# Landmark phase as a three-stage pipeline over images with 32-row score tiles

## What is computed

```
x = x + lstm(group_norm(x))
t = tokens(x)
a = layer_norm(t);  xn = layer_norm(a) * gamma + beta
q, k, v = split(xn @ w_qkv)
q_l, k_l = means of q and k over 64 segments of 64 tokens
out = softmax(q k_l') @ pinv(softmax(q_l k_l')) @ (softmax(q_l k') @ v)
out = (out + depthwise_conv(v)) @ w_out + b_out
t = t + a + out
t = t + ffn_recurrence(layer_norm(t))
```

## Time and profile before

| | us |
|---|---|
| median of three runs | 7382.85 (7371.74 to 7390.95) |
| the profiled execution's own time | 7392.79 |
| its span | 7391.1 |
| landmark phase, 1612 to 3246 us of the span | 1634 |
| pinv phase, to 3628 us | 382 |
| output phase, to 5060 us | 1432 |
| recurrence, to the end | 2331 |

### The profile page before, as it was taken

The page is one execution under the profiler, slowest core; times in us unless marked ns, Lnnn a source line. Parts: engine busy times, 40 slices in busy tenths (PEclk is TensorE's granted clock), DMA queues, the critical chain, the costliest instruction groups (busy, mean ns, idle before and its releaser), DMA issues. The chain is left out here.

```text
span 7391.1 us, 234424 instructions
## 1 busy us (share of the span) xinstructions
PE 6762.3 (91%) x93297; PEld 3741.3 (51%) x93297; DVE 3505.2 (47%) x9371; ACT 3435.6 (46%) x9744; POOL 1775.4 (24%) x1718
## 2 busy tenths in 40 slices
PE   4599999978888898889899999997999999999999
PEld 3499888973333343459544444443333333333333
DVE  7677777767667777734266666662000000000000
ACT  4465555655555555524355555553333333333333
POOL 1000000015666766630044444441000000000000
PEclk6799999988999999989899999998999999999999
DMA  6521111233444433310144444442111111111111
GB/s 273 231 95 68 69 69 46 93 108 123 138 138 138 138 128 119 98 51 0 54 154 151 153 152 147 152 138 62 42 52 52 41 54 41 52 41 52 45 50 41
DMA packets 749351, 711.30 MB, mean 96 GB/s; under 512 B 61168, under 2 KB 655088, under 8 KB 741104
## 3 DMA queue, kind: packets, MB, share of 16 engines
q1 hardware_dynamic: 733872, 594.91, 25.7%
q0 software_dynamic: 14400, 101.45, 3.4%
HBM read 388.50 MB, written 305.80 MB: 94 GB/s over the span
## 5 line engine op out<-in xcount | busy, mean ns | idle before, releaser
L2060 PE MATMUL f_junk<-f_idle 128*32 128x384 bf16 x24736 | 1565.1, 323 | 1.5 <-issue 1.3
L2103 ACT ACTIVATE f_y<-f_acc 128x16 f32<-128x16 f32 x4096 | 753.7, 184 | 1555.6 <-PE f_acc L2071 1555.5
L2071 PEld LDWEIGHTS f_acc<-f_y,f_vT 128*32 128x32 f32 x32768 | 649.2, 108 | 1415.0 <-ACT f_y L2103 1403.2
L2071 PE MATMUL f_acc<-f_y,f_vT 128*32 128x16 f32 x32768 | 1049.6, 193 | 60.7 <-issue 12.2
L2018 DVE TENSOR_TENSOR f_sum<-f_turned,f_t 128x512 f32<-128x512 f32 x128 | 88.6, 692 | 1769.0 <-PE f_turned L2053 1768.9
L695 POOL TENSOR_TENSOR a_acc<-a_acc,a_p 128x512 f32<-128x512 f32 x480 | 617.5, 1287 | 350.2 <-ACT a_p L898 345.4
L898 ACT ACTIVATE a_p<-a_s 128x512 f32<-128x512 f32 x512 | 300.5, 590 | 638.8 <-PE a_s L826 596.0
L825 PE MATMUL a_s<-a_ws,a_xnT 128*128 128x512 f32 x1024 | 568.8, 638 | 22.3 <-issue 19.8
L1789 DVE TENSOR_REDUCE o_m<-o_bank_l 128x8 f32<-128x512 f32 x512 | 326.1, 679 | 413.7 <-PE o_bank_l L1591 413.5
L2060 PEld LDWEIGHTS f_junk<-f_idle 128*32 128x32 bf16 x24736 | 446.4, 96 | 3.6 <-issue 3.6
L999 DVE TENSOR_REDUCE a_m3p<-a_l 128x1 f32<-128x512 f32 x512 | 319.1, 684 | 143.7 <-PE a_l L766 141.8
(11 more groups left out here) (251 smaller groups left out, 13385.4 us busy)
## 6 DMA issues: line engine op xcount, KB each, us to landing
a_hid<-hidden SPq DMA_DIRECT2D x16, 4127.5 KB, 13.4
hidden<-l_h POOLq DMA_DIRECT2D x48, 1040.0 KB, 6.3
skew<-gn_skew POOLq DMA_DIRECT2D x8, 6144.0 KB, 23.8
l_x<-skew SPq DMA_DIRECT2D x48, 1024.0 KB, 5.2
gn_x<-in_x SPq DMA_DIRECT2D x16, 2048.0 KB, 12.3
a_xin<-in_x SPq DMA_DIRECT2D x128, 256.0 KB, 6.7
base<-a_t SPq DMA_DIRECT2D x16, 2048.0 KB, 8.8
xnt<-a_xnT SPq DMA_DIRECT2D x16, 2048.0 KB, 14.0
```

The lines of the kernel that those rows point to most:

```text
L2060: nc.tensor.matmul(junk[rows, :], idle[:, 0:QUAD], idle[:, :], start=True, stop=True)
L2071: mm = nc.tensor.matmul(acc[k % 2][rows, t, :], vT[:, rows], before, start=False, stop=True, skip_group_check=True)
L2103: nc.scalar.activation(y[q][:, u, :], acc[u // RC % 2][:, u % RC, :], ACT.Sigmoid).then_inc(s_y, 1)
```

## The change

`landmark_phase` is rewritten. Time is cut into `B + 2` = 18 periods of eight slots, and three images are in work at once. In period `p`, slot `c`, group `c` of image `p` is added and normalised (its transposes, keys and values are one slot later), the landmarks and the rounded maxima belong to image `p-1`, and the scores, exponentials and weighing to image `p-2`.

- Keys are now formed (`keys`, one 512-column float32 product per group) and kept as `kT`. A score is a product over the 32 channels of two heads: four tiles of 32 rows, one for each pair of heads, each into its own bank. A group takes 4 bf16 products for the shift and 16 float32 products of 128 columns. The product `w_k @ qbd` and the four-row shift are gone.
- The values are stored 17 wide per head with a one in the last place, so that a row of the weighing is the softmax's sum. POOL's adding into `acc` is gone. The weighing has 8 products of 64 columns per tile (before: 4 of 128).
- The norm is made by POOL alone (five operations, two of 512 elements), which also keeps `gain` and `loss` for each tile. DVE's L936, L937, L946, L951, L952 and ACT's L876 and POOL's L682 are gone; `tokens` (the unscaled `t`) goes to memory in place of `base`. POOL also rounds the keys; ACT's L870 is gone.
- The two transposes share one bank `turn` (before: two), keys and values share `proj`, and the rounded products and all small landmark products share one bank `L` (before: two banks and `misc`).
- Transfers are cut into groups of 512 tokens and eight pieces of the hidden rows, each issued in its slot by SP.
- In `output_phase`, the add of `base` (one 128x512 operation) becomes four operations of 128 columns with `gain`, a wait, and four with `loss` and `b_out`. The convolution reads its values 17 apart.

The core of the diff follows (marks of removed lines are left out for `landmark_phase`, whose old text stands above).

```diff
+        LAST = {1: 0, 2: 6, 3: 12, 4: 18, 5: 23, 6: 28, 7: 32}
+        ROUNDED = {1: range(0, 3), 2: range(3, 4), 3: range(4, 5), 4: range(5, 7), 5: range(7, 8)}
...
+        def before(p, c):
+            return (p, c - 1) if c else (p - 1, NG - 1)
...
+            def slot(p, c, q):
+                more = valid(p + 1)
+                if valid(p):
+                    if c in (1, 3, 5) and more:
+                        load_hidden(p + 1, c // 2)
+                    if c == NG - 1 and more:
+                        for piece in range(3, 8):
+                            load_hidden(p + 1, piece)
+                    if c + 3 < NG:
+                        load_x(p, c + 3)
+                    elif more:
+                        load_x(p + 1, c + 3 - NG)
+                i, d = before(p, c)
+                if valid(i):
+                    store_normed(i, d)
+                if valid(p):
+                    store_tokens(p, c)
+                if valid(i):
+                    store_values(i, d, q if c else 1 - q)
...
+            def norm(i, c):
+                n = nth(i, c) - 1
+                mean = mv[c % 2][:, :, 0]
+                var = mv[c % 2][:, :, 1].unsqueeze(1).broadcast_to([P, 2, GT])
+                wait(pool, "bn", n + 1)
+                pool.tensor_tensor(vare[:, :, :], var, coef[:, :, :], ALU.mult).then_inc(s["pow"], 1)
+                pool.wait_ge(s["pow"], 6 * n + 1)
+                pool.tensor_tensor(vare[:, :, :], vare[:, :, :], plus[:, :, :], ALU.add).then_inc(s["pow"], 1)
+                wait(pool, "xt", n)
+                pool.tensor_tensor(xn[:, :, :], t[c % 2][:, :, :], mv[c % 2][:, :, 0:1].broadcast_to([P, GT, C]), ALU.subtract
+                                   ).then_inc(s["pow"], 1)
+                pool.wait_ge(s["pow"], 6 * n + 3)
+                pool.tensor_tensor(r[:, :, :], vare[:, :, :], half[:, :, :], ALU.pow).then_inc(s["pow"], 1)
+                pool.wait_ge(s["pow"], 6 * n + 4)
+                pool.tensor_tensor(xn[:, :, :], xn[:, :, :], r[:, 1, :].unsqueeze(2).broadcast_to([P, GT, C]), ALU.mult
+                                   ).then_inc(s["xn"], 1)
+                tiles = slice(GT * c, GT * c + GT)
+                pool.tensor_tensor(R.gain[:, bass.ds(i, 1), tiles], r[:, 0:1, :], one[:, :].unsqueeze(2).broadcast_to([P, 1, GT]),
+                                   ALU.add).then_inc(s["pow"], 1)
+                pool.tensor_tensor(R.loss[:, bass.ds(i, 1), tiles], r[:, 0:1, :], mean.unsqueeze(1), ALU.mult
+                                   ).then_inc(s["pow"], 1)
+            def round_keys(i, j, q):
+                wait(pool, "kc", nth(i, j))
+                wait(pool, "lp", NL * i + PAIRS_H * (j - 2) if j >= 3 else NL * i)
+                pool.tensor_tensor(k_lp[j % 3][:, :], kT[q][:, 512 * j:512 * j + 512], one[:, :].broadcast_to([C, 512]), ALU.mult
+                                   ).then_inc(s["rk"], 1)
+            def slot(p, c, q):
+                if valid(p):
+                    norm(p, c)
+                if valid(p - 1):
+                    for j in ROUNDED.get(c, ()):
+                        round_keys(p - 1, j, 1 - q)
+            each_period(pool, slot)
...
+            def turn_hidden(i, c):
+                wait(pe, "hc", nth(i, c))
+                if isinstance(i, int) and nth(i, c) == 2:
+                    wait(pe, "add", 1)
+                wait(pe, "xnT", nth(i, c) - 2)
                 for k in range(GT):
+                    mt = nc.tensor.transpose(turn[:, k, :], hrow[c % 2][:, P * k:P * k + P], R.ident[:, :])
+                mt.then_inc(s["ht"], 1)
+            def turn_normed(i, c):
+                wait(pe, "xn", nth(i, c))
+                wait(pe, "add", min(nth(i, c) + 1, NG * B) if isinstance(i, int) else nth(i, c) + 1)
                 for k in range(GT):
...
+            def keys(i, c):
+                wait(pe, "xnT", nth(i, c))
+                wait(pe, "valc", nth(i, c) - 1)
+                nc.tensor.matmul(proj[:, :], w[:, C:2 * C], xnT[c % 4][:, :], start=True, stop=True).then_inc(s["km"], 1)
+            def values(i, c):
+                wait(pe, "kc", nth(i, c))
+                for k in range(GT):
+                    mt = nc.tensor.matmul(proj[:, P * k:P * k + P], xnT[c % 4][:, P * k:P * k + P], w[:, 2 * C:3 * C],
+                                          start=True, stop=True)
+                mt.then_inc(s["vm"], 1)
...
+            def rounded_scores(i, j):
+                if j % PAIRS_H == 0:
+                    wait(pe, "rk", NG * i + j // PAIRS_H + 1)
                 if j == 0:
...
+            def turn_maxima(i):
+                wait(pe, "set", SET * i + 11)
+                nc.tensor.transpose(L[:, 0:P], m3[:, :], R.ident[:, :]).then_inc(s["lm"], 1)
+            def scores(i, c, q):
+                wait(pe, "exp", PAIRS_H * (nth(i, c) - 1))
+                if c == 0:
+                    wait(pe, "set", SET * (i + 1))
+                for g in range(PAIRS_H):
+                    rows = slice(QUAD * g, QUAD * g + QUAD)
+                    nc.tensor.matmul(S[g][:, :], sel[rows, :], m3row[q][rows, :].unsqueeze(1).broadcast_to([QUAD, GT, P]),
+                                     start=True, stop=False)
                 for k in range(GT):
+                    at = 512 * c + P * k
+                    for g in range(PAIRS_H):
+                        rows = slice(QUAD * g, QUAD * g + QUAD)
+                        ms = nc.tensor.matmul(S[g][:, P * k:P * k + P], kT[q][rows, at:at + P], qbd[q][rows, P * g:P * g + P],
+                                              start=False, stop=k == GT - 1)
+                ms.then_inc(s["s"], 1)
+            def weigh(i, c, q):
+                wait(pe, "exp", PAIRS_H * nth(i, c))
+                if c == 0:
+                    wait(pe, "ctx", CTX * (i - 1) + 1)
+                for k in range(GT):
+                    for h in range(2):
+                        for g in range(PAIRS_H):
+                            at = VROW * (GT * c + k) + (DH + 1) * (2 * g + h)
+                            mw = nc.tensor.matmul(pv[QUAD * g:QUAD * g + QUAD, LM * h:LM * h + LM], v[q][:, at:at + QUAD],
+                                                  p3[c % 2][g][:, P * k + LM * h:P * k + LM * h + LM],
+                                                  start=c == 0 and k == 0 and h == 0, stop=c == NG - 1 and k == GT - 1,
+                                                  skip_group_check=True)
+                mw.then_inc(s["pvd"], 1)
+            def context(i):
+                wait(pe, "ctx", CTX * i + 1)
+                nc.tensor.transpose(L[:, 0:P], pvs[:, :], R.ident[:, :]).then_inc(s["turnc"], 1)
+            def slot(p, c, q):
+                i, d = before(p, c)
+                due = list(range(LAST.get(c - 1, 0), LAST.get(c, 0))) if valid(p - 1) else []
+                def rounded():
+                    if due:
+                        rounded_scores(p - 1, due.pop(0))
+                if valid(p - 2):
+                    scores(p - 2, c, q)
+                if c == 1 and valid(p - 1):
+                    landmarks(p - 1)
+                rounded()
+                if valid(p):
+                    turn_hidden(p, c)
+                rounded()
+                j, e = before(p - 2, c)
+                if valid(j):
+                    weigh(j, e, q if c else 1 - q)
+                rounded()
+                if valid(i):
+                    turn_normed(i, d)
+                rounded()
+                if c == 0 and valid(p - 3):
+                    context(p - 3)
+                if valid(i):
+                    keys(i, d)
+                rounded()
+                if valid(i):
+                    values(i, d)
+                rounded()
+                if c == 1 and valid(p - 1):
+                    landmark_scores(p - 1, 1 - q)
+                if c == NG - 1 and valid(p - 1):
+                    turn_maxima(p - 1)
...
+            def copy_normed(i, c):
+                wait(act, "xt", nth(i, c))
+                stored(act, s_stx, nth(i, c) - 4)
+                wait(act, "xm", nth(i, c) - 4)
+                wait(act, "vm", nth(i, c) - 4)
+                nc.scalar.activation(xnT[c % 4][:, :], turn[:, :, :].rearrange("c k t -> c (k t)"), ACT.Identity,
+                                     bias=bet[:, 0:1], scale=gam[:, 0:1]).then_inc(s["xnT"], 1)
+            def copy_keys(i, c, q):
+                wait(act, "km", nth(i, c))
+                wait(act, "s", nth(i - 2, c))
+                wait(act, "rk", nth(i - 2, c))
+                nc.scalar.activation(kT[q][:, 512 * c:512 * c + 512], proj[:, :], ACT.Identity).then_inc(s["kc"], 1)
+            def copy_values(i, c, q):
+                wait(act, "vm", nth(i, c))
+                wait(act, "pvd", nth(i - 2, c))
+                stored(act, s_stv, nth(i - 2, c))
+                nc.scalar.activation(v[q][:, GT * VROW * c:GT * VROW * (c + 1)].rearrange("p (a d) -> p a d", d=DH + 1)[:, :, 0:DH],
```

(81 more changed lines are left out.)

665 lines of the change are left out of this document (221 added, 444 removed).

## The result

The changed kernel takes 7435.53 us, median of four runs (7419.61 to 7437.80), against 7381.83 (7371.74 to 7390.95, four runs) for the kernel before: a ratio of 1.0068 [1.0049, 1.0088]. It is 0.7% slower, where 7223 us was predicted. The profiled execution took 7435.45 us, its span 7433.7.

What follows compares the result with a forecast made beforehand. PE was taken to bound the landmark phase, a chain over all engines the output phase's slots. From 7392.8 us, -314 (landmark) and +154 (output) gave 7233 profiled, 7223 as median; range 7010 to 7370 us.

Steps and rivals of the forecast that it cites:

- landmark phase: Landmark phase: all periods with opening and closing sum to 1320 us against 1634 before, 314 less.
- two blocks, delay only: Output phase: two blocks for the add make `z` later, slots 11.6 us instead of 10.41, +154 us over 127 slots.
- the forecast 75%: Sign in the landmark phase: PE's busy share near 75%.
- the opening and the closing: Ends of the landmark phase: opening 13 us, period 16 52, period 17 and tail 38; good to some 20 us together.
- the sum that gave 78: Landmark image: 73.8 us of slots plus two clock falls, each losing about 2 us, make 78 us.
- the walk: Landmark image followed slot by slot through its waits: slots of 8.65 to 11.8 us, slot 0 7.8, together 73.8 us.
- the power and the masked queries: Landmark slots 1 and 2: POOL's power with eight elements taken as 2.2 us, DVE's L987 as 1.80.
- two falls an image: Landmark phase: PE's waiting brings the clock to 1.2 GHz twice per image, each fall losing about 2 us.
- The rival in which the waits don't bind: Landmark phase: signals overlap better, PE sets the pace, 64 us per image, about 7027 us; chance 0.18.
- that rival: Landmark scores: row tiles of 128 columns don't overlap, 4.4 us for 0.96, about 7600 us; chance 0.04.
- POOL's terms: Landmark slot: POOL's norm operations, power, four small ones and one rounding, given as 6.3 us.
- its rival there: Landmark phase: low clock holds; all periods at 1.2 GHz give 116 us per image, 7755; half the time or more, chance 0.11.

Runs made afterwards that it cites:

- experiment 7: Changed kernel with four unread products ahead of PE's wait for `z`, and `gain` and `loss` always those of image 0 (constant addresses): 7228.32 us.
- 1: Changed kernel with the output phase's residual again one add of 128x512, `gain`, `loss` and `b_out` left out: 7053.41 us.
- experiment 3: Changed kernel with four bf16 products that nobody reads ahead of PE's wait for `z`: 7250.82 us.
- experiment 4: Kernel before, its add of base replaced by two blocks of four operations with constants one and zero: 7659.09 us.
- 5: Kernel before with its add replaced by two blocks with constants one and zero, plus four unread products ahead of the wait for `z`: 7558.70 us.
- 8: Changed kernel with `gain` and `loss` always those of image 0 (constant addresses), no unread products ahead of the wait: 7310.38 us.
- experiments 10 to 12: Changed kernel with base made early (7051.41 us), and maxima over 256 of 512 columns, two of four tiles weighed, or both: 7032.60, 7047.45, 6990.52 us.

## Why the prediction was wrong

Against its own steps, in us, from profiled execution to profiled execution:

| step | predicted | measured |
|---|---|---|
| landmark phase | -314 | -350 |
| two blocks, delay only | +154 | +175 (experiment 7 less 1) |
| addresses ahead of the blocks | none | +22 (experiment 3 less 7) |
| clock in the output phase | none | +185 (changed kernel less 3) |
| rest, by difference | 0 | +11 |
| sum, from 7392.8 us | -160 | +43 |

**The landmark phase was right in its mechanism, and its number in part by luck.** PE is no longer the bound: it is busy for 74% of the time (785 of 1063 us), near the forecast 75%, at a clock of 0.95. The slots came out at 8.5 to 9.7 us, predicted 8.65 to 8.9 for those of four to six maxima. Of the 36 us by which the phase is shorter than forecast, the thirteen full images make 40 (75.0 us for 78); the opening and the closing came out within 3 us of their terms. In the loop an image takes 77.7 us from its first scores to the next image's (mean of eight), but not by the sum that gave 78. An image with neither a fall of the clock nor the loop's end takes 71.0 us, where the walk had 73.8; the power and the masked queries, taken 1.7 us too dear in all, are likely the most of it. The clock falls 10 times in the eight images, where two falls an image were put in. And the pause at the loop's end, some 5 us an image (last section), had no term. The rival in which the waits don't bind (64 us) was 11 us too low. The row tiles overlap, so that rival fell too.

**The delay was right but for its size.** The durations of the blocks were exact (2.33 us for the add's 0.73 is 1.60 more, 1.58 taken), and what the blocks alone added to the median slot is 11.77 - 10.50 = 1.27 us, predicted 1.2. The term left out that DVE forms addresses for operands that are picked by the image. These instructions aren't in the timeline and don't count as busy; they show as longer distances between `project`, the first block and the second. Two sums slipped without weight: 127 x 1.2 is 152, not 154, and POOL's terms add up to 6.1 us, not 6.3.

**The step that failed is the clock.** "All of the chain shifts: ... the slot is 11.6 us instead of 10.41, 1.2 more." This takes PE's work in the slot as unchanged at both sides of the wait. The clock was weighed in the landmark phase alone, where PE's share falls, and its rival there did not come true. In the output phase the new wait turned a phase with 17 waits for `z` and 7 falls into one with a pause in each slot, and the clock fell 118 times. A fall costs about 1.6 us: 185 us for 112 falls between experiment 3 and the changed kernel, 100 us for 61 between experiments 4 and 5, 82 us for 50 between 8 and 7. The windows and the timeline of the slot show where: at 1.2 GHz the transposes of `z` take 0.97 us for 0.65 and the scores 1.92 for 1.03, `project` starts 1.26 us later in the slot, and with it the whole chain to the next `z`. So the slot pays for the fall in full: the wait for `z` doesn't take it up, and comes again whether or not the clock fell (1.65 us in the quiet slot of experiment 4).

The rows to see it by were there. The slot of 10.41 us has no wait of PE but 0.21 us (its end in the earlier trace rows), and the earlier trace rows show a stretch with PE busy for 1.89 of 3.40 us being followed by 1.2 GHz. A slot with some 1.2 us of waiting in 11.6 was neither, and should have been given the low clock as a case with its own price. The Trainium skill (TensorE: Matmul & The Clock Gate, A second HAM failure mode: psum-queue depth-cycling) says that in another kernel frequent short idles between groups of products made the clock go up and down. The runs here agree in part: 118 falls where the median wait was 1.74 us, but 6 with 0.89 us of idling, as few as without the wait.

**What stays open.** Which slots of experiments 4 and 8 begin a group of falls, and why about half of all keep 2.4 GHz with waits of the same length, no run tells. The 11 us of rest are about the 0.09 us by which a slot with the plain add (10.50) is over that of the earlier trace rows, 127 times; what causes them, the values 17 apart or something else, wasn't tried alone. What else sets a landmark slot's pace, beside the two paths of experiments 10 to 12, was not found.

## What to carry to other kernels

Work added to a chain that PE waits for in every round costs its delay less the slack, and then perhaps as much again: if the wait is new, give TensorE's clock a term of its own in that stage, priced by what the work behind the wait takes at half the clock. Before adding operations behind a wait, ask what can be made ahead of it: here the same arithmetic, with even more time on DVE, cost nothing at the start of the slot and 382 us between `project` and `z`. Filling a wait with products that nobody reads brought back about half of the loss, moving the work brought back all of it.

## What the runs showed that was not expected

- The clock answers very unevenly to small differences in waiting: 128 waits of 231 us in all go with 118 falls, 202 us with 57, and waits partly filled, down to 0.89 us of idling, with the 6 or 7 of the undisturbed kernels.
- Addresses formed from a loop's register ahead of each of eight operations take 0.34 us of the median slot if they stand behind a wait (12.11 against 11.77 us; 0.23 of the mean), and the timeline shows no operation for them.
- A multiplication of 128x512 on DVE took 1.80 us in the kernel before and 0.68 us in the changed one. The traces show what goes with it: in 15 of the 16 images before, POOL was busy beside it nearly all the time (L682, L695) and it took 1.80; in the first image before (but for 0.03 us) and in all 16 after, POOL was idle beside it and it took 0.68.
- At the end of every second landmark image, where the loop's body ends, PE stands still for about 6 us with no releaser, and the other engines start nothing for over 4 us of it. Here with the first product of the next pass of the loop:

```profile
2194.21 0.27 PE L794 MATMUL a_l<-r_ident,a_m 128*128 128x128 f32 x1
2200.46 0.61 PE L804 MATMUL a_s<-a_m3row,a_sel 32*128 32x512 bf16 x4 [5.98 <-issue]
```

The images come in turns of about 72 and 82 us by it, so it is worth some 5 us per image. Ten packets of the kind `instruction` are in flight from 2190 to 2203 us, so that engines wait there for their next instructions is likely; it wasn't tried.
